# Dot attention, denominators: GpSimd adds up head 0 only, VectorE all of head 1

## What is computed

```python
q = x1.reshape(n, HEAD_SIZE, -1).transpose(1, 0, 2) * SCALE
k = x2.reshape(n, HEAD_SIZE, -1).transpose(1, 0, 2)
vv = v.reshape(n, HEAD_SIZE, -1).transpose(1, 0, 2)
scores = jnp.einsum('hnd,hmd->hnm', q, k)
scores = jnp.where(adj > 0, scores, NEG_FILL)
attn = jax.nn.softmax(scores, axis=-1)
out = jnp.einsum('hnm,hmd->hnd', attn, vv)
...
x = _layernorm(x + _L1_gnn_ref(x, L1_gnn_x2, L1_gnn_v, adj), axis=-1)
```

## Time and profile before

| | us |
|---|---|
| median of 3 executions | 4285.08 (4284.36 to 4285.78) |
| the profiled execution | 4283.16 |
| its span, first to last instruction | 4281.7 |
| dot attention, first matmul to last copy | 2009.1 to 4119.2 |
| mean granted TensorE clock | 0.942 of full |

### The profile page before, as it was taken

The page is one execution under the profiler, slowest core; times in us unless marked ns, Lnnn a source line. Parts: engine busy times, 40 slices in busy tenths (PEclk is TensorE's granted clock), DMA queues, the critical chain, the costliest instruction groups (busy, mean ns, idle before and its releaser), DMA issues. The chain is left out here.

```text
span 4281.7 us, 56011 instructions
## 1 busy us (share of the span) xinstructions
PE 3923.2 (92%) x19321; PEld 1350.7 (32%) x19321; DVE 3373.5 (79%) x3190; ACT 2534.9 (59%) x2396; POOL 2194.8 (51%) x987
## 2 busy tenths in 40 slices
PE   7887999999999999866999999999999999999977
PEld 5563222222222222253322222322223222223235
DVE  5556999999999999786877777877778777777756
ACT  3445888888888888612555555555555555555520
POOL 3331000000000000054999999999999999999940
PEclk9998999999999999866999999999999999999975
DMA  7884111111111111265111111111111111111133
GB/s 273 281 288 141 40 49 45 38 39 40 49 45 40 37 49 45 69 231 148 36 46 47 46 47 42 40 47 47 47 40 40 47 47 47 46 44 38 38 109 138
DMA packets 266187, 323.91 MB, mean 76 GB/s; under 512 B 21056, under 2 KB 193088, under 8 KB 266048
## 3 DMA queue, kind: packets, MB, share of 16 engines
q1 hardware_dynamic: 238400, 262.89, 20.1%
q0 software_dynamic: 10496, 33.83, 2.2%
q10 hardware_dynamic: 17152, 25.43, 1.7%
HBM read 262.70 MB, written 59.38 MB: 75 GB/s over the span
## 5 line engine op out<-in xcount | busy, mean ns | idle before, releaser
L1128 POOL TENSOR_TENSOR a_pool_total<-a_pool_total,a_weights 128x1024 f32<-128x1024 f32 x704 | 1861.3, 2644 | 104.1 <-POOL a_pool_total L1128 3.2
L1109 DVE TENSOR_TENSOR a_weights<-a_psS,maskT 128x1024 f32<-128x1024 f32 x1024 | 1203.8, 1217 | 506.7 <-ACT a_psS L1076 291.6
L1076 ACT ACTIVATE a_psS<-a_psS,a_shift 128x1024 f32<-128x1024 f32 x1024 | 1078.9, 1085 | 866.3 <-PE a_psS L1005 865.8
L477 ACT ACTIVATE g_weights<-al_bc,g_shift,g_xl 128x1024 f32<-128x1024 f32 x1024 | 1187.8, 1231 | 167.4 <-DVE g_total L523 81.8
L516 DVE TENSOR_TENSOR g_weights<-g_weights,maskT 128x1024 f32<-128x1024 f32 x1024 | 1176.0, 1222 | 97.2 <-ACT g_weights L477 96.0
L1005 PE MATMUL a_psS<-a_q,a_k 128*128 128x512 f16 x4096 | 1000.3, 384 | 66.9 <-DVE a_weights L1109 48.4
L1022 PE MATMUL a_psO<-a_weights,a_v 128*64 128x512 f32 x4096 | 988.5, 605 | 0.0
L568 PE MATMUL g_psO<-g_weights,g_xl 128*64 128x512 f32 x4096 | 966.1, 603 | 17.2 <-DVE g_weights L516 17.2
L599 POOL DMA_DIRECT2D o_scratch<-g_o x16 | 8.9, 556 | 1387.8 <-ACT g_d L486 1387.8
L1005 PEld LDWEIGHTS a_psS<-a_q,a_k 128*128 128x128 f16 x4096 | 351.4, 98 | 892.0 <-DVE a_weights L1109 272.7
L568 PEld LDWEIGHTS g_psO<-g_weights,g_xl 128*64 128x64 f32 x4096 | 259.3, 136 | 701.7 <-issue 403.3
(11 more groups left out here) (131 smaller groups left out, 1767.2 us busy)
## 6 DMA issues: line engine op xcount, KB each, us to landing
adj_sb<-in_adj_dram SPq DMA_DIRECT2D x128, 512.0 KB, 5.3
g_xl<-xl_scratch SPq DMA_DIRECT2D x128, 260.0 KB, 2.9
a_k<-k_scratch SPq DMA_DIRECT2D x256, 128.0 KB, 3.0
a_v<-in_L_gnn_v_dram SPq DMA_DIRECT2D x128, 256.0 KB, 2.9
al_bc<-alpha_scratch SPq DMA_DIRECT2D x16, 1024.0 KB, 5.0
f_oT<-o_scratch SPq DMA_DIRECT2D x16, 1024.0 KB
a_q<-q_scratch SPq DMA_DIRECT2D x64, 256.0 KB, 5.0
xl_scratch<-xl_sb POOLq DMA_DIRECT2D x32, 260.0 KB, 4.3
```

The lines of the kernel that those rows point to most:

```text
L477: nc.scalar.activation(w[:, u % NP, h, :], al_bc[:, par, h, :], ACT.Exp, bias=shift_bc[:, par, h:h + 1], scale=xl[:, slot, u % KB, 2 * C + ...
L1076: nc.scalar.activation(psS[n % RING][:], psS[n % RING][:], ACT.Exp, bias=shift_bc[:, g % 2, h:h + 1], scale=SCALE).then_inc(exped, 1)
L1109: nc.vector.tensor_tensor(w[:, u % NP, h, :], psS[n % RING][:].rearrange("p a c -> p (a c)"), maskT[:, j, (g // PAIRS) * IC:(g // PAIRS + ...
L1128: pool.tensor_tensor(pool_total[:, h, :], other, w[:, u % NP, h, :], ALU.add).then_inc(pool_added, 1)
```

## The change

GpSimd's list loses every addition of head 1, `pool_total` shrinks to one head, and VectorE's list gets all of head 1: an addition behind the two masks of each step, of the step two before (`add(u - 2)`), instead of one behind every second step, of the step one before. TensorE's denominators read one total per head, so four matmuls in place of six. One function `adds_by` counts for both semaphores. A mask of head h waits only for the engine that adds up head h.

```diff
-        pool_total = sb("pool_total", [P, 2, IC], F32)
+        pool_total = sb("pool_total", [P, IC], F32)
...
-        def pool_adds_by(u):
+        def adds_by(u):
             g, j = divmod(u, NT)
-            return g * (NT - 1 + NT // 2 - 1) + j + max(j // 2, 0)
-
-        def dve_adds_by(u):
-            g, j = divmod(u, NT)
-            return g * (NT // 2 - 1) + max((j + 1) // 2 - 1, 0)
+            return g * (NT - 1) + j
...
-                for h in range(2):
+                for h, total in enumerate((pool_total, dve_total)):
                     for hf in range(2):
                         row = 32 * (2 * h + hf)
                         last = nc.tensor.matmul(psO[row:row + 32, 0, :], onesF[:, 0:32],
-                                                pool_total[:, h, hf * HALF:(hf + 1) * HALF], start=True, stop=(h == 0))
-                for hf in range(2):
-                    row = 32 * (2 + hf)
-                    last = nc.tensor.matmul(psO[row:row + 32, 0, :], onesF[:, 0:32],
-                                            dve_total[:, hf * HALF:(hf + 1) * HALF], start=False, stop=True)
+                                                total[:, hf * HALF:(hf + 1) * HALF], start=True, stop=True)
...
+                    dve.wait_ge((pool_added, dve_added)[h], adds_by(freed + 1 if freed % NT == 0 else freed))
...
-                if u > 0 and (u - 1) % NT % 2 == 1 and (u - 1) % NT >= 3:
-                    add(u - 1)
-            add(GROUPS * NT - 1)
+            for u in range(GROUPS * NT):
+                mask(u, 0)
+                mask(u, 1)
+                if u >= 2 and (u - 2) % NT > 0:
+                    add(u - 2)
+            for u in range(GROUPS * NT - 2, GROUPS * NT):
+                add(u)
...
-                if j >= 1:
-                    add(u, 0)
-                if j >= 2 and j % 2 == 0:
-                    add(u, 1)
+                pool.wait_ge(masked, 2 * u + 1)
+                pool.tensor_tensor(pool_total[:], other, w[:, u % NP, 0, :], ALU.add).then_inc(pool_added, 1)
```

More of the change, by code:

```diff
@@ L1028, in denominators @@
                 pe.wait_ge(o_taken, g + 1)
-                pe.wait_ge(pool_added, pool_adds_by((g + 1) * NT - 1))
-                pe.wait_ge(dve_added, dve_adds_by((g + 1) * NT - 1))
-                for h in range(2):
+                pe.wait_ge(pool_added, adds_by((g + 1) * NT - 1))
+                pe.wait_ge(dve_added, adds_by((g + 1) * NT - 1))
+                for h, total in enumerate((pool_total, dve_total)):
                     for hf in range(2):
@@ L1089, in add, with mask @@
                 dve.wait_ge(masked, 2 * u + 2)
-                if j == 3:
+                if j == 1:
                     if g > 0:
                         dve.wait_ge(d_summed, g)
-                    other = w[:, (u - 2) % NP, 1, :]
+                    other = w[:, (u - 1) % NP, 1, :]
                 else:
-                    dve.wait_ge(dve_added, dve_adds_by(u - 2))
+                    dve.wait_ge(dve_added, adds_by(u - 1))
                     other = dve_total[:]
                 nc.vector.tensor_tensor(dve_total[:], other, w[:, u % NP, 1, :], ALU.add).then_inc(dve_added, 1)
+            def mask(u, h):
+                g, j = divmod(u, NT)
+                n = 2 * u + h
+                dve.wait_ge(exped, n + 1)
+                if u >= NP:
+                    freed = u - NP
+                    dve.wait_ge(w_used, freed + 1)
+                    dve.wait_ge((pool_added, dve_added)[h], adds_by(freed + 1 if freed % NT == 0 else freed))
+                nc.vector.tensor_tensor(w[:, u % NP, h, :], psS[n % RING][:].rearrange("p a c -> p (a c)"),
+                                        maskT[:, j, (g // PAIRS) * IC:(g // PAIRS + 1) * IC],
+                                        ALU.mult).then_inc(masked, 1)
@@ L1099, in _ @@
+            for u in range(GROUPS * NT):
[5 more added lines that the diff above has]
+                add(u)
+        @block.gpsimd
+        def _(pool):
             for u in range(GROUPS * NT):
                 g, j = divmod(u, NT)
[L1101 to L1111, removed]
@@ L1112, in _ @@
-                if u > 0 and (u - 1) % NT % 2 == 1 and (u - 1) % NT >= 3:
-                    add(u - 1)
-            add(GROUPS * NT - 1)
[L1116 to L1121, removed]
+                if j == 0:
+                    continue
+                pool.wait_ge(masked, 2 * u + 1)
+                if j == 1:
                     if g > 0:
@@ L1123, in add @@
                         pool.wait_ge(d_summed, g)
-                    other = w[:, (u - 1 - h) % NP, h, :]
+                    other = w[:, (u - 1) % NP, 0, :]
                 else:
[L1126 to L1131, removed]
-                if j >= 1:
-                    add(u, 0)
-                if j >= 2 and j % 2 == 0:
-                    add(u, 1)
+                    pool.wait_ge(pool_added, adds_by(u - 1))
@@ L1138, in attend_with_maximum @@
+                    other = pool_total[:]
+                pool.tensor_tensor(pool_total[:], other, w[:, u % NP, 0, :], ALU.add).then_inc(pool_added, 1)
 def attend_with_maximum(nc, sem, layer, adj, xl_dram, al_dram, v, x1_dram, x2, o_dram, d_dram, identF):
```

## The result

| | us |
|---|---|
| before, median of 4 executions | 4284.83 (4284.36 to 4285.78) |
| changed, median of 4 executions | 4516.45 (4514.21 to 4517.58) |
| ratio, with 95% interval | 1.054 (1.0521 to 1.0558) |
| predicted | 4519 (4450 to 4630) |
| span of the profiled execution, before and changed | 4281.7 and 4514.4 |

The account below looks back on a forecast made before the run. The prediction took GpSimd as the bound before, and in the changed kernel VectorE waiting for GpSimd's additions: 4.65 us steps, 146.1 us groups. The copy comes 233.7 us later, added to 4285.1: about 4519 us, range 4450 to 4630.

Parts of the forecast that it names:

- The bound before: Dot attention before the change: GpSimd bounds, groups 131.3 us apart against 118.4 at TensorE's pace, 12.9 us more.
- The meeting: Each step: VectorE's addition finds GpSimd adding and ends 1.08 us after it, taking 2.46 us; a step takes 4.65.
- the sum: Whole kernel: 432 steps of 4.65 us, passages between groups and the end; copy 233.7 us later, about 4519 us.
- No backlog on GpSimd: Steps of the changed kernel: one GpSimd addition of 2.35 us each, under 3.5 with waiting, so any backlog melts.
- Between groups: Passage from one group to the next: five steps take 20.5 us, 27 take 125.6; 146.1 us per group against 131.3.
- The end: After the last step's mask: a meeting, two more VectorE additions, denominators at 8.5 us where it was 19.5; saves 11.
- The start: First steps of the dot attention stay as they are; the 4.65 us step holds from the masks at 2022.06.
- The range: Errors of 0.1 us per step (43 us) and 3 us between groups (45): 4450 to 4590; with the clock's case 4630.
- The clock: TensorE in the dot attention: busy 3.70 of 4.65 us, idle 0.95 per step, clock at 1.00 also between groups.
- The rival in which the clock falls: TensorE's idle time in each step lowers its clock: about 105 us more, 4625 us; chance 8%.
- The rival of the other sign: VectorE adds before GpSimd, TensorE's 3.70 us step bounds, a group about 121 us: 4120 us; chance 11%.

Follow-up runs that it names:

- the cut to 768 columns: Kernel before, with GpSimd's additions cut to the first 768 of 1024 columns in both heads: 4101.2 us, groups 120.1 us apart instead of 131.3.
- the versions that meet the condition: Changed kernel with VectorE's addition between its two masks, 4090.6 us; changed kernel with GpSimd's addition also waiting for the mask of head 1, 4096.95 us.

## Why the prediction was right

Its range held the time, and its forecast is 2.5 us from the median. By its steps:
- **The bound before.** GpSimd, with 12.9 us per group over TensorE's pace: shown by the cut to 768 columns, where 11.2 of them go. The other 1.7 I put down to GpSimd wrongly: TensorE is busy in them too, with the matmuls of the denominators, which a group has beside its 32 steps of 3.70.
- **The meeting.** 1.30, 2.35 and 1.08 were read off one meeting in the first group; the changed kernel repeats it in step after step with 1.29, 2.36 and 1.08. Predicted 2.46 us for VectorE's addition and 4.65 for the step, measured 2.460 and 4.65: from mask to mask of head 0, 448 steps of the stage are 4.64 to 4.66 long: the 432 of the sum, the 15 from the last tile of a group to the next group, which the sum has in the passage, and the one before them all, at j = 3 of the first group. The Trainium skill's rule of a full block ("SBUF — State Buffer", section "Who interferes with whom"), read strictly with 1.22 behind GpSimd's end, would have made the addition 2.60; the trace has 2.46.
- **No backlog on GpSimd.** It waits for VectorE's mask for about 2.3 us in each step. The view of waits over the whole execution (total, times, longest) has 450 such waits. By the timeline 433 of them are 2.29 or 2.30 us long: before the addition in each of the 432 steps that follow a step of the sum, and once more at j = 4 of the first group. At j = 4 of the other 15 groups it waits 0.5, just after catching up, and two waits come with the very first additions:

```profile
POOL a_pool_total L1125 <- DVE a_weights L1099: 1024.3, 450, 21.1
```

- **Between groups.** 146.1 us predicted, 145.8 measured. From the last step's mask to that of j = 4 I had 20.5 and the trace has 20.28 (2446.23 to 2466.51). Over 15 groups the sum has 4.5 us too much.
- **The end.** I had 8.5 us from the last step's mask to the copy of the denominators; it was 9.5 (4342.08 to 4351.59). The last denominators ran at half clock: their rows of two matmuls are 1.07 us long where those between groups have 0.62. TensorE had been idle for 3.19 us, waiting for the last of VectorE's additions, and the granted clock went to 0.50, the 1.2 GHz level, at 4348.8. The first row is from VectorE's timeline, the second from TensorE's:

```profile
4344.34 5.11 DVE L1089 TENSOR_TENSOR a_dve_total<-a_dve_total,a_weights 128x1024 f32<-128x1024 f32 x3
...
4349.60 1.07 PE L1030 MATMUL a_psO<-a_pool_total,onesF 128*32 128x512 f32 x2 [3.19 <-DVE a_dve_total L1089]
```

- **The start.** I took the start of the stage as it was. In this profiled execution its first matmul came at 2011.42 instead of 2009.12, after the unchanged stages. That is +2.3; with -4.5 and +1.0 it makes -1.2, and the sum comes to 232.5 of the 232.7 us by which the spans differ. Each of the three is small; that they nearly cancel is luck.
- **The range.** Its two errors, 43 and 45 us, added to 4519 make 4431 to 4607, not the 4450 to 4590 that the text has for them. The measured time is well inside either.
- **The clock.** TensorE's idle time per step was 0.78, I had 0.95, and the granted clock, at 0.50 when the stage begins, was at full from 2014.1 to 4348.8. The rival in which the clock falls did not come: in 432 steps with 0.78 us of idle time it never did. By the section of the Trainium skill named there ("TensorE: Matmul & The Clock Gate", "A second HAM failure mode: psum-queue depth-cycling") short idle times between groups of matmuls made the clock of another kernel swing; this trace doesn't show it at 0.78 us.
- **The rival of the other sign** had its mechanism right and its condition, VectorE first, unmet. Its gain was put a little too low: I gave 121 us for a group and 4120 for the time, and the versions that meet the condition have 119.2 and 119.5 and 4091 and 4097. The passage between groups costs TensorE about 0.8 to 1.1 us over 32 steps, where I had put 2.6. That is about what the four matmuls of the denominators take by themselves, 1.00 from start to the next scores; the rest of the passage costs TensorE next to nothing.

## What to carry to other kernels

Adding up busy times of two engines says nothing when their instructions exclude each other. Here the two additions do. The masks don't: their mean in the changed kernel is 1.210 us, though GpSimd adds from 1.29 to 3.65 us of each step and the mask of head 1 runs until 2.34. By plain sums each engine had room to spare (77 and 108 of 118.4 us per group), and yet the kernel was 5% slower. Look for what starts each of the two, let the engine on the critical chain ask first, and let the other wait with its longer instruction; here either swapping two instructions on VectorE or holding GpSimd back by one semaphore count brought 9% over the changed kernel, and 4.5% over the one before. A moved piece of work is judged by the moment at which it now stands, so try its neighbours in the list before giving the move up.

## What the runs showed that was not expected

The whole difference hangs on some 1 us: VectorE asking 0.98 us after GpSimd costs 4516 us, asking 0.16 us before it 4091 to 4097, and neither order slides into the other: 448 steps are 4.64 to 4.66 us long with the one, and 448 are 3.70 with each of the other two. Cutting GpSimd's instruction by a quarter took 1.811 us where three quarters of 2.354 are 1.766; from 1024 to 512 columns it is 2.12 ns per column with some 0.19 us that don't depend on size.
